# Half tiles between whole tiles, three sums instead of four, dense blocks in the tiles' rotation

## The reference, cut to what matters

```python
x = x + jnp.tanh(g_xattn[0]) * _L0_xattn_ref(ctx_512, _layernorm(x), W, b)
x = x + jnp.tanh(g_ffn[0])   * _L0_ffn_ref(_layernorm(x), ...)

def _L0_ffn_ref(x, ...):             # H=256, M=176, E=32 experts, 6 of 32 per token
    scores = sigmoid(xf @ w_router); sfc = scores + corr_bias
    # the 4 best of 8 groups of experts, then the 6 best experts of those
    combine = zeros((T, E)).at[rows, topk_idx].add(topk_w)
    g = einsum('th,ehm->etm', xf, gate_w); u = einsum('th,ehm->etm', xf, up_w)
    eo = einsum('etm,emh->eth', silu(g) * u, down_w)
    routed = einsum('te,eth->th', combine, eo)
    shared = silu(xf @ sh_gate_w) * (xf @ sh_up_w) @ sh_down_w
    return routed + shared
```

## Time and profile before

| | us |
|---|---|
| median of 3 runs | 234.37 |
| lowest, highest | 232.65, 234.91 |
| the profiled execution: its time | 234.94 |
| the profiled execution: its span | 233.1 |
| PE busy in the span | 208.0 (89%) |
| DVE, POOL (GpSimd), ACT busy | 128.9, 125.1, 74.0 |

### The profile page before, as it was taken

How to read it: one execution, slowest core, us unless ns; L and a number is a source line. 1 busy time by engine, 2 the same in 40 slices (tenths; PEclk the granted TensorE clock), 3 DMA queues, 4 the chain that set the end, 5 groups by cost and what they waited for, 6 DMA issues and landing times.

```text
span 233.1 us, 4430 instructions
## 1 busy us (share of the span) xinstructions
PE 208.0 (89%) x1021; PEld 154.3 (66%) x1022; DVE 128.9 (55%) x518; ACT 74.0 (32%) x204; POOL 125.1 (54%) x131
## 2 busy tenths in 40 slices
PE   6999699999679999978899969999998999799950
PEld 6888388888457786756677747777775544357730
DVE  2699988989975544323343432434435555313895
ACT  3608212111011123231533333443443545343210
POOL 6326387777777773554516256667567575540000
PEclk9659999999999999999999979999999999889997
DMA  6999999999999995999999967577755544348955
GB/s 200 269 275 229 388 356 344 316 367 308 362 300 365 313 381 178 220 249 247 212 298 300 317 126 117 101 136 118 114 105 90 64 50 50 44 46 243 325 179 180
DMA packets 40243, 51.78 MB, mean 222 GB/s; under 512 B 4894, under 2 KB 34942, under 8 KB 40214
## 3 DMA queue, kind: packets, MB, share of 16 engines
q1 hardware_dynamic: 26192, 31.44, 44.9%
q0 software_dynamic: 8960, 14.97, 30.2%
q10 hardware_dynamic: 5062, 5.03, 8.0%
HBM read 30.69 MB, written 20.74 MB: 221 GB/s over the span
## 4 chain that ended last, share of the span: by engine, by line
PE 55%; DVE 20%; DMA 11%; issue 5%; ACTq 4%; ACT 3%; DVEq 1%; POOL 1%; POOLq 0%
PE pG L855 11%; DMA sums_dram<-choice,idx 9%; PE pY L869 7%; PE pG L979 5%; PE pG L917 4%; PE pG L779 4%; PE pY L928 3%; PE pH L863 3%; PE pG L796 3%; PE pY L890 3%; PE pX L849 3%; DVE xs L1428 2%; PE pY L999 2%; PE pY L790 2%; ACTq L285 2%
## 5 line engine op out<-in xcount | busy, mean ns | idle before, releaser
L499 POOL DMA_INDIRECT sums_dram<-choice,idx x42 | 65.1, 1551 | 54.9 <-DMA sums_dram<-choice,idx 25.0
L488 POOL DMA_INDIRECT rows_dram<-rows,row_i x48 | 47.4, 988 | 19.1 <-issue 14.1
L855 PE MATMUL pG<-wgu,sdown 128*128 x136 | 47.0, 468 | 5.3 <-ACT sdown L604 5.3
L869 PE MATMUL pY<-wd,sup 88*128 x136 | 35.9, 387 | 0.0
L1320 DVE COPY sup<-pH 88x256 f32<-88x256 f32 x42 | 17.6, 418 | 32.9 <-PE pH L863 31.5
L855 PEld LDWEIGHTS pG<-wgu,sdown 128*128 128x128 f32 x136 | 23.6, 193 | 13.7 <-issue 6.4
L617 ACT ACTIVATE choice<-pY,wt 128x256 f32<-128x256 f32 x34 | 16.1, 474 | 45.9 <-PE pY L869 13.3
L869 PEld LDWEIGHTS pY<-wd,sup 88*128 88x128 f32 x136 | 23.6, 194 | 2.0
L863 PEld LDWEIGHTS pH<-ident,sgate 128*88 128x88 f32 x84 | 12.8, 163 | 13.0 <-issue 4.7
L1316 DVE TENSOR_TENSOR sgate<-sgate,pG 128x176 f32<-128x176 f32 x42 | 13.7, 326 | 9.3 <-ACT sgate L609 9.3
L609 ACT ACTIVATE sgate<-pG 128x176 f32<-128x176 f32 x42 | 13.3, 317 | 14.3 <-PE pG L855 11.0
(11 more groups left out here) (225 smaller groups left out, 341.2 us busy)
## 6 DMA issues: line engine op xcount, KB each, us to landing
wgu<-in_L_ffn_gate_w_dram SPq DMA_DIRECT2D x8, 704.0 KB, 10.7
wgu<-in_L_ffn_up_w_dram SPq DMA_DIRECT2D x8, 704.0 KB, 11.1
wd<-in_L_ffn_down_w_dram SPq DMA_DIRECT2D x8, 640.0 KB
rows<-rows_dram ACTq DMA_DIRECT2D x22, 144.5 KB, 4.0
rows_dram<-zeros SPq DMA_DIRECT2D x8, 289.0 KB, 4.2
sums_dram<-zeros POOLq DMA_DIRECT2D x2, 1152.0 KB, 13.2
sums_dram<-zeros SPq DMA_DIRECT2D x2, 1152.0 KB, 8.7
rows<-sums_dram SPq DMA_DIRECT2D x8, 256.0 KB, 4.0
```

Source lines behind the costliest of these rows:

```text
L488: pool.indirect_dma_start(rows_dram[:, :], bass.IndirectOffsetOnAxis(ap=row_i[:, j, k:k + 1], axis=0), rows[:, j, :], None).then_inc(done, 16)
L499: pool.indirect_dma_start(pair_dram[u % 2][:, :], bass.IndirectOffsetOnAxis(ap=idx[:, u % ROUND:u % ROUND + 1], axis=0), y[u % YRING], Non ...
L855: ins = nc.tensor.matmul(pG[par][:, 0:2 * M].rearrange("t (g m) -> t g m", g=2), xT[:, par, k, :], wgu[:, bass.ds(e, 1), :, k, :].rearrang ...
L869: ins = nc.tensor.matmul(pY[par][:, 0:H], hT[0:MI, par, i, :], wd[:, bass.ds(e, 1), i, :], start=(i == 0), stop=(i == I - 1))
```

## The change

The order of the expert work, the number of sums and who adds them change; what is computed stays the same.

- **Half tiles between whole tiles.** There are 42 steps now. Half tiles take the even steps 18 to 32 (`DUO_STEPS`, from `MID` on), whole tiles the rest. In the step after a half tile, PE does `turn_x`, `turn_h`, and then the half tile's gate and up and the earlier half tile's down next to each other. Their loads are issued by SP (`load_duo`): the first two before SP waits for the last weights, the others after the late zeroing.
- **Three sums.** All half tiles fall on even steps, so only the even tensor needs a second copy. SP sets one sum to zero late where it set two, and GpSimd waits for that before the add of step 18. The sum of the lower halves (sum 1) is complete after step 32 and is read back then, two parts at once and two when the last rows have been transposed.
- **Dense blocks in the rotation.** The last whole tile and the dense blocks overlap as two tiles do; the branch on extra rounds stands ahead of this.
- **GpSimd adds on chip.** DVE adds ten parts where it added 16: four of sum 1 and two of sum 0 during the dense blocks, four at the end. The two other parts of sum 0 are added by GpSimd (`tensor_tensor`, 128 x 512) to the parts of sum 2 that have arrived, and DVE adds these.

```diff
-SUMS = 4
-EARLY = SUMS // 2
+SUMS = 3
+MID = LEAD + 14
...
+    STEPS = PLAIN + DUOS
+    DUO_STEPS = range(MID, MID + 2 * DUOS, 2)
+    COLUMN = list(itertools.accumulate((n not in DUO_STEPS for n in range(STEPS)), initial=0))
...
+    PARTS_READ = [(1, b) for b in range(B)] + [(0, b) for b in range(B)] + [(2, 2), (2, 3), (2, 0), (2, 1)]
+    PAIRED = [2, 3]
+    PARTS_ADDED = [(1, b) for b in range(B)] + [(0, 0), (0, 1), (2, 0), (2, 1), (2, 2), (2, 3)]
+    PARTS_BY = [2, 4, 4, 4, 4, 4, 6, len(PARTS_ADDED)]
...
-        pair_dram = [nc.dram_tensor(f"sums{i}_dram", [2 * (T + P), H], F32, kind="Internal").ap() for i in range(SUMS // 2)]
-        sums_dram = [pair_dram[i // 2][i % 2 * (T + P):(i % 2 + 1) * (T + P), :] for i in range(SUMS)]
+        even_dram = nc.dram_tensor("even_dram", [2 * (T + P), H], F32, kind="Internal").ap()
+        odd_dram = nc.dram_tensor("odd_dram", [T + P, H], F32, kind="Internal").ap()
+        sums_dram = [even_dram[0:T + P, :], even_dram[T + P:2 * (T + P), :], odd_dram]
...
+
+            def load_duo(p):
+                n = DUO_STEPS[p]
+                sp.wait_ge(s_xT, n - (XRING - 1))
+                sp.wait_ge(s_taken, n - (XRING - 1))
+                for a, there in enumerate((s_lower[p], s_load[n % XRING])):
+                    v = sp.value_load(tiles[1:2, DUO_AT + 2 * p + a:DUO_AT + 2 * p + a + 1], min_val=0,
+                                      max_val=4 * (E // 2 * PAIR - HALF) + SEGS - 1)
+                    at = v >> 2
+                    sp.dma_start(xg[n % XRING][a * HALF:(a + 1) * HALF, :],
+                                 rows_dram[bass.ds(at, HALF), :]).then_inc(there, 16)
+
+            load_duo(0)
+            load_duo(1)
             for n in range(24 - FLOW, 24):
                 weights_there(n)
-
-            for i in range(EARLY):
-                sp.dma_start(sums_dram[2 * i + 1].rearrange("(j p) c -> p j c", p=P),
-                             zeros[:, 0:H].unsqueeze(1).to_broadcast([P, J + 1, H])).then_inc(s_clear_late, 16)
+            sp.dma_start(sums_dram[1].rearrange("(j p) c -> p j c", p=P),
+                         zeros[:, 0:H].unsqueeze(1).to_broadcast([P, J + 1, H])).then_inc(s_clear_late, 16)
+            for p in range(2, DUOS):
+                load_duo(p)
+
+            def read_part(part):
+                i, b = PARTS_READ[part]
+                sp.dma_start(parts[part % len(parts)],
+                             sums_dram[i][0:T, :].rearrange("(j p) c -> p j c", p=P)[:, b * HALVES:(b + 1) * HALVES, :]
+                             ).then_inc(s_sums[i][b], 16)
+
+            sp.wait_ge(s_y, DUO_STEPS[-1] + 1)
+            sp.wait_ge(*added(0, DUO_STEPS[-1]))
+            for part in range(IN_ROWS):
+                read_part(part)
             rounds = load_rounds(sp)
             with sp.If(rounds > HELD):
                 with sp.Fori(HELD, ROUNDS) as i:
                     with sp.If(i < rounds):
                         for s in range(ROUND):
-                            load(sp, i * ROUND + (LEAD + s), LEAD + s, all_placed=True)
-            for p in range(DUOS):
...
+                            load(sp, i * ROUND + (LEAD + DUOS + s), LEAD + DUOS + s, all_placed=True)
+            end = LEAD + DUOS
+            sp.wait_ge(s_xT, rounds * ROUND + end)
...
-            sp.wait_ge(s_taken, rounds * ROUND + (LEAD + DUOS))
+            sp.wait_ge(s_taken, rounds * ROUND + end)
...
+            for part in range(IN_ROWS, B):
+                read_part(part)
+            for part in range(B, SUMS * B):
+                if part % B == 0:
+                    sp.wait_ge(*added(rounds, end - 3 + part // B))
+                    sp.sem_inc(s_passed, 1)
+                if part == IN_CHOICE:
+                    sp.wait_ge(*added(rounds, end - 1))
+                    sp.sem_inc(s_passed, 1)
+                if part >= len(parts):
+                    sp.wait_ge(s_summed, part - len(parts) + 1)
+                read_part(part)
...
-            for t in range(PLAIN):
-                add(0, t)
+            for n in range(STEPS):
+                if n == MID:
+                    pool.wait_ge(s_clear_late, 16)
+                add(0, n)
...
-            pool.wait_ge(s_clear_late, 16 * (SUMS - EARLY))
-            for p in range(DUOS):
-                add(rounds, LEAD + p)
+                            add(i, LEAD + DUOS + s)
+            for b in PAIRED:
+                for i in (0, 2):
+                    pool.wait_ge(s_sums[i][b], 16)
+                even, odd = (parts[PARTS_READ.index((i, b))] for i in (0, 2))
+                pool.tensor_tensor(out=odd, in0=odd, in1=even, op=ALU.add).then_inc(s_paired, 1)
...
-            for t in range(2, PLAIN):
+            for t in range(2, STEPS):
                 copy_xT(t, t % 2)
                 silu(t - 1, (t - 1) % 2)
                 for n in [n for n in FETCH if FETCH[n] == t - 2]:
                     load(act, n, n)
                 if t >= 3:
                     scale_y(0, t - 3)
+                if t - 2 in DUO_STEPS:
+                    copy_down_duo(DUO_STEPS.index(t - 2))
...
+            def place_filled(n):
+                pe.wait_ge(s_load[n % XRING], 16 * (n // XRING + 1))
+                if n in DUO_STEPS:
+                    pe.wait_ge(s_lower[DUO_STEPS.index(n)], 16)
...
-            for t in range(2, PLAIN):
-                transpose_x(t % XRING, t // XRING + 1, t % 2)
-                e_of[t - 1] = look_up(t - 1)
-                pe.wait_ge(s_ready, e_of[t - 1] + 1)
-                gate_up(t - 1, (t - 1) % 2, e_of[t - 1])
-                turn_h(t - 2, t % 2)
-                if t >= 3:
+            for t in range(2, STEPS):
+                place_filled(t)
+                turn_x(t % XRING, t % 2)
+                if t - 1 in DUO_STEPS:
+                    turn_h(t - 2, t % 2)
+                    gate_up_duo(t - 1, (t - 1) % 2, DUO_STEPS.index(t - 1))
+                else:
+                    e_of[t - 1] = look_up(COLUMN[t - 1])
+                    pe.wait_ge(s_ready, E if t > MID else e_of[t - 1] + 1)
+                    gate_up(t - 1, (t - 1) % 2, e_of[t - 1])
+                    turn_h(t - 2, t % 2)
+                if t - 3 in DUO_STEPS:
+                    p = DUO_STEPS.index(t - 3)
+                    down_duo(t - 3, (t - 3) % 2, p, look_up(DUO_AT + 2 * p))
+                elif t >= 3:
                     if t <= 4:
                         pe.wait_ge(s_byc, J - 4 + t)
                     take_down(t - 3, (t - 3) % 2, e_of.pop(t - 3))
...
-            first = rounds * ROUND + LEAD
-            e_end = None
-            for p in range(DUOS + 2):
-                if p < DUOS:
-                    at, there = loaded_duo(rounds, p)
-                    pe.wait_ge(at, there)
-                    turn_x((LEAD + p) % XRING, p % 2)
-                if p == 0:
-                    e_end = look_up(first - 1)
-                    gate_up(first - 1, 1, e_end)
-                elif p <= DUOS:
-                    gate_up_duo(first + (p - 1), (p + 1) % 2, p - 1)
-                turn_h(first + p - 2, p % 2)
-                if p < 3:
-                    take_down(first + p - 3, (p + 1) % 2, e_end if p == 2 else look_up(first + p - 3))
-                else:
-                    down_duo(first + (p - 3), (p + 1) % 2, p - 3, look_up(DUO_AT + 2 * (p - 3)))
+                            take_down(t - 3, (u - 3) % 2, e_by.pop(u - 3) if u - 3 in e_by else look_up(column - 3))
+            first = rounds * ROUND + (LEAD + DUOS)
+            column = rounds * ROUND + LEAD
+            e_common = pe.value_load(busy_i[0:1, 1:2], min_val=0, max_val=E - 1)
...
-            e_common = pe.value_load(busy_i[0:1, 1:2], min_val=0, max_val=E - 1)
+            e_end = look_up(column - 1)
+            gate_up(first - 1, 1, e_end)
+            turn_h(first - 2, 0)
+            take_down(first - 3, 1, look_up(column - 3))
             gate_up_common(0)
-            e_end = look_up(DUO_AT + 2 * (DUOS - 1))
-            pe.wait_ge(s_yc, first + (DUOS - 2))
-            down_duo(first + (DUOS - 1), (DUOS - 1) % 2, DUOS - 1, e_end)
-            for j in range(J):
+            turn_h(first - 1, 1)
+            take_down(first - 2, 0, look_up(column - 2))
+            gate_up_common(1)
+            turn_h_common(0)
+            take_down(first - 1, 1, look_up(column - 1))
+            for j in range(1, J):
                 if j + 1 < J:
                     gate_up_common(j + 1)
                 turn_h_common(j)
-                if j:
-                    down_common(j - 1)
+                down_common(j - 1)
             down_common(J - 1)
...
-            for t in range(2, PLAIN):
+            for t in range(2, STEPS):
                 copy_hT(t - 2, t % 2)
                 gate(t - 1, (t - 1) % 2)
-                take(0, t - 1)
+                if t - 1 in DUO_STEPS:
+                    take_duo(DUO_STEPS.index(t - 1))
+                else:
+                    take(0, t - 1)
```

(49 more changed lines are left out.)

106 lines of the change are left out of this document (31 added, 75 removed).

## The result

The changed kernel takes 238.69 us (median of 4 runs, 237.86 to 240.75), the kernel before 233.98 (median of 4) in the same comparison: ratio 1.0242, 95% interval 1.0175 to 1.0309. It is slower; whether by a full 2%, the interval leaves open. 222.7 was forecast, in a range of 219.5 to 229.0. The profiled execution took 238.39 us, span 236.3.

The account below looks back on a forecast made before the run. PE's program was taken to set the pace. Gains of 3.8 (zeroing), 1.0 (half tiles), 4.3 (dense blocks, net of branch) and 2.6 (end) took 234.94 to 223.2 us profiled, 222.7 as median; range 219.5 to 229.0.

Parts of the forecast that it names:

- What bounds the kernel: From tile 17 to dense block 7, PE's program sets the pace, with 2.49 us per plain step and 2.27 per dense step.
- Do the other engines keep up with a pair: Whole plus half tile steps: PE needs 5.3 us, DVE 3.5, so DVE keeps up and its weight copy is covered.
- slack of 1.8 us: DVE's spare time in a pair of steps, claimed to cover its copy of the next half tile's weights.
- The rival of longer pairs: Pairs of steps: shape changes not saved or DVE's copy in PE's way, 0.36 to 0.53 us a half tile; chance 0.13.
- Half tiles at +0.32: Half tiles between whole tiles: two shape changes each on PE cost +0.32 us, 2.6 instead of 3.6, a gain of 1.0.
- The branch at 1.0: Branch on extra rounds, between the last two whole tiles: still costs 1.0 us, bounds 0 and 1.1.
- The zeroing at 3.8: Steps behind tile 17: one late zeroing instead of two removes the whole loss of 3.8 us, bounds 0 and 3.8.
- The rival of the late zeroing: Behind tile 17: the late zeroing still collides with adds, the 3.8 us loss stays, 226.5 us; chance 0.17.
- The end: From dense block 7's gate-up to the span's end: 10.4 us instead of 13.03, gain 2.6, bounds 0 and 3.7.
- GpSimd's addition: Each of GpSimd's two 128 x 512 additions at the end takes about 1 us, hidden.
- The blocking rival: At the end, DVE and GpSimd additions wait for each other, DVE's chain grows up to 2 us, 224.7; chance 0.08.
- The sum: Gains of 9.1 us from tile 17 to dense block 2 and 2.6 at the end, 11.7 off the profiled execution.

Follow-up runs that it names:

- e8: e3 with ACT's copy of the half tile's down weights moved ahead of its row load and scaling of y; 230.85 us, ratio 0.976 to the kernel before.
- e1: Changed kernel with PE reading the half tile's expert into a register ahead of the wait for the rows; 235.04 us, ratio 0.9966 to the kernel before.
- e2: Changed kernel with DVE's three register loads for half tiles moved ahead of its wait for SiLU; 235.9 us, ratio 1.0068 to the kernel before.
- e3: Changed kernel with the edits of both e1 and e2; 235.43 us, ratio 0.9911 to the kernel before.
- e12: Changed kernel, branch kept, but everything behind it takes the number of rounds as a constant; 238.97 us, one run.
- e7: e8, e5 and e6 joined, the whole computation with the branch kept; 227.54 us, ratio 0.9648 to the kernel before.
- e6: Changed kernel with the third sum's late zeroing issued early by GpSimd instead of SP; 239.61 us, ratio 1.0173 to the kernel before.
- e10: Changed kernel with all twelve additions on DVE and none on GpSimd; 241.23 us, ratio 1.0307 to the kernel before.
- e11: e8, e4 and e6 joined, so without the branch and extra rounds; 226.43 us, ratio 0.9631 to the kernel before.
- e14: Changed kernel with PE's loop of extra rounds holding one tile instead of ten, so a shorter jump; 236.04 us, one run.
- e15: Changed kernel with only PE's branch and loop left out, the other engines keeping theirs; 234.12 us, one run.
- e19: e11 run once more, unchanged; 227.4 us, one run.
- e5: Changed kernel, branch kept, with PE's five register loads around it made in the plain steps before; 236.72 us, ratio 1.0127 to the kernel before.
- e4: Changed kernel without the branch and extra-round loops on all engines, number of rounds constant; 234.53 us, ratio 1.0075 to the kernel before.

## Why the prediction was wrong

- **What bounds the kernel.** Right for before, and again for e8, where PE is full. Wrong for the changed kernel, which a ring of waits bounds.
- **"Do the other engines keep up with a pair."** This is the step that failed. DVE's 3.5 us of need against 5.3 us, "slack of 1.8 us", is a sum of busy time, and the copy of weights was said to be covered by it. What counts is the path: the half tile's gate-up, SiLU, gate, three register loads, the copies, the whole tile's gate, turn_h, one more load on PE, the next gate-up. It measures 6.49 us. Of the 8.3 us that this cost, e1, e2, e3 and e8 give back all but 0.3: 5.35 against 5.30. The rival of longer pairs had the copy's place right, but its 0.36 to 0.53 a half tile came from changes of shape that aren't saved or from the copy's own 0.53, without the loads around it; 1.19 was measured.
- **Half tiles at +0.32.** Right, in e8, where nothing else binds: 2.81 for a step with change of shape, 2.54 for the next.
- **The branch at 1.0.** A term mis-sized: 5.53 - 2.27 = 3.3 us in the changed kernel, and up to 4.3 in e12, for PE's jump and the two register loads behind it. I had read the cost off a place where ACT was late and took the jump for hidden. It was short there: the branch took 0.39 us, and the last 16 KB transfer of q8 had landed at 166.84, 4.7 us ahead of it. That the target lay in instructions already fetched fits this; no run shows it.
- **The zeroing at 3.8.** Also mis-sized: a loss of 2.2 stood in its place. The rival of the late zeroing came true in part: an add still landed 7.1 us after its issue. Part of the loss seems to be the ring's (e8, loads moved and zeroing late, 3.68), part the zeroing that is left (e7, both, 2.81; e6 3.18). How much is whose can't be said closer, since this step scatters by over 1 us among runs with the late zeroing.
- **The end.** Right: 10.58 for 10.4, and e10 shows what GpSimd's help is worth, 1.2. GpSimd's addition: 1.25 us for about 1. The blocking rival had the mechanism right, but in the changed kernel the additions miss each other; it came true in e11, e14, e15 and e19.
- **The sum.** With loads and copies out of the ring, the zeroing early and the branch away, 69.9 us against 70.1 were measured (e11): the units were nearly right, the claim that nothing else binds wasn't. Part of the agreement is luck, since the 70.1 contain 1.0 for a branch that e11 lacks; e7, which has it, took 71.76. e11's profiled execution still takes 226.43 us and not 223.2, since tile 17 began at 131.06 instead of 129.48 and the end cost 1.8 more.

## What to carry to other kernels

When steps of two kinds alternate, write down the path from one step to the next of its kind through all engines, in program order and with register loads, before busy time is summed; slack in busy time doesn't shorten it. Read registers ahead of a wait, not behind it, and put the copy that the next matmul needs ahead of loads and scalings that can wait. Behind a jump over a long unrolled loop nothing of that engine runs ahead: make the register loads that follow it before the jump (e5, e7), and keep the code that it jumps over short (e14).

## What was not expected of the hardware

A register load costs about half a microsecond where nothing covers it: two of them fill the time from 144.20, when DVE's gate ends, to 145.23, and one is TensorE's 0.67 us of issue at 148.16 in the chain above; e1 took that one out of the ring and won 0.35 to 0.53 a pair. After the long jump PE often ran on at half its clock. The table by stretch of e12, from the end of the idle time to dense block 0, then the next step:

```profile
205.37:210.00 4.63, 4.63 (x10) 3.12 (x11) 1.00 (x4) 0.32 (x1) 0.59 (x1) 0.50 0.25 28
210.00:212.44 2.44, 2.44 (x11) 1.86 (x10) 0.66 (x2) 0.79 (x2) 0.95 (x1) 0.93 0.65 191
```

The granted clock is 0.50 (1.2 GHz) after 4.15 us of idle time, gate-up takes 2.71 us instead of 1.35, and the step after the jump 4.63 instead of 2.27. In eight of the eleven traces with the long jump the granted clock of this step was 0.50 to 0.61, after idle times of 2.84 us (e10) and 3.11 (e1) too. In the changed kernel's own profile, where the idle time was 3.10, it stayed at 1.00; what decides this is open. In e5 and e7, with 1.84 and 1.60 us of idle time, it was 1.00 as well. With the loads behind it and the slower clock, the long jump thus costs 3.4 us (changed kernel) to 6.7 (e12), both steps together less the 4.53 of e4.
